# A graph attention layer: the products of V moved to GpSimd, the first body reordered, the last body finished block by block

## The reference

```python
h  = maximum(layernorm(x), 0)
Wh = h @ W
e  = leaky_relu((Wh @ a[:64])[:, None] + (Wh @ a[64:])[None, :], 0.2)
scores    = where(adj > 0, e, -9e15)
attention = softmax(scores, axis=1)
out = x + elu(attention @ Wh)
```

## Time and profile before, and how to read it

| | us |
|---|---|
| median of 3 runs | 683.38 |
| the profiled execution's own time | 682.71 |
| its span, first to last instruction | 680.8 |
| TensorE / VectorE / ScalarE / GpSimd busy | 632.8 / 616.9 / 630.5 / 60.2 |
| DMA | 275.16 MB, mean 404 GB/s |

### The profile page before, as it was taken

How to read it: one execution, slowest core, us unless ns; L and a number is a source line. 1 busy time by engine, 2 the same in 40 slices (tenths; PEclk the granted TensorE clock), 3 DMA queues, 4 the chain that set the end, 5 groups by cost and what they waited for, 6 DMA issues and landing times.

```text
span 680.8 us, 23844 instructions
## 1 busy us (share of the span) xinstructions
PE 632.8 (93%) x10422; PEld 620.1 (91%) x10422; DVE 616.9 (91%) x625; ACT 630.5 (93%) x366; POOL 60.2 (9%) x51
## 2 busy tenths in 40 slices
PE   4769999999998999999999999989898998989895
PEld 4648899999998999999999999989898998989895
DVE  6999899999989899889999999898989989898993
ACT  5998899999999998999999999989898998989981
POOL 5000101011010101011010201010010101001020
PEclk9969999999999999999999999999999999999999
DMA  9997899999999999999999999999999999999970
GB/s 320 426 426 286 328 420 410 422 427 427 428 424 430 428 425 425 429 428 425 427 425 429 428 425 428 426 427 426 427 427 426 427 427 428 425 427 428 424 301 19
DMA packets 24841, 275.16 MB, mean 404 GB/s; under 512 B 3088, under 2 KB 7440, under 8 KB 8432
## 3 DMA queue, kind: packets, MB, share of 16 engines
q1 hardware_dynamic: 22864, 270.67, 94.5%
q0 software_dynamic: 1488, 4.07, 1.6%
q10 hardware_dynamic: 464, 0.07, 0.1%
HBM read 272.70 MB, written 2.10 MB: 404 GB/s over the span
## 4 chain that ended last, share of the span: by engine, by line
DMA 32%; DVE 24%; ACT 20%; PE 14%; issue 10%; DVEq 1%; SPq 0%; ACTq 0%
DMA adj_ring<-in_adj 31%; DVE code L675 15%; ACT work L514 14%; PE psum L916 5%; PE psum L914 5%; ACT work L522 3%; DVE work L688 3%; PE psum L896 3%; DVE code L682 1%; PE psum L954 1%; DMA work<-in_x 1%; ACT trow L497 1%; DVE last_steps L706 1%; DVE last_steps L710 1%; DVE last_steps L699 1%
## 5 line engine op out<-in xcount | busy, mean ns | idle before, releaser
L916 PE MATMUL psum<-V,work 128*128 128x130 f16 x4096 | 492.1, 221 | 0.0
L914 PE MATMUL psum<-V,work 128*128 128x130 f16 x4096 | 491.7, 219 | 0.4 <-DVE work L688 0.4
L514 ACT ACTIVATE work<-trow,Wh 128x4096 int8<-128x4096 f32 x128 | 477.0, 3727 | 1.6 <-DVE code L682 1.6
L914 PEld LDWEIGHTS psum<-V,work 128*128 128x128 fp8e4 x4096 | 400.9, 98 | 0.5 <-issue 0.5
L916 PEld LDWEIGHTS psum<-V,work 128*128 128x128 fp8e4 x4096 | 398.0, 97 | 0.0
L675 DVE TENSOR_SCALAR code<-adj_ring 128x4096 uint8<-128x4096 int32 x128 | 293.0, 2290 | 26.4 <-DMA adj_ring<-in_adj 25.2
L682 DVE SCALAR_TENSOR_TENSOR code<-work,code 128x1024 int32<-128x1024 int32 x128 | 156.5, 1223 | 9.9 <-ACT work L514 7.5
L896 PE MATMUL psum<-identb,code 128*128 128x128 bf16 x2048 | 136.8, 221 | 24.2 <-DVE code L682 20.9
L522 ACT COPY work<-psum 128x1024 int32<-128x1024 int32 x128 | 129.9, 1015 | 26.2 <-PE psum L896 26.2
L896 PEld LDWEIGHTS psum<-identb,code 128*128 128x128 bf16 x2048 | 120.0, 98 | 29.9 <-DVE code L682 21.3
L688 DVE TENSOR_SCALAR work<-work 128x1024 int32<-128x1024 int32 x128 | 88.0, 687 | 3.3 <-ACT work L522 3.2
(11 more groups left out here) (76 smaller groups left out, 150.7 us busy)
## 6 DMA issues: line engine op xcount, KB each, us to landing
adj_ring<-in_adj SPq DMA_DIRECT2D x128, 2048.0 KB, 16.5
work<-in_x SPq DMA_DIRECT2D x4, 512.0 KB, 6.1
last_steps<-in_x POOLq DMA_DIRECT2D x16, 128.0 KB, 6.8
out_y<-last_steps POOLq DMA_DIRECT2D x15, 128.0 KB, 7.8
out_y<-last_steps SPq DMA_DIRECT2D x1, 128.0 KB, 1.9
W<-in_L_gnn_W ACTq DMA_DIRECT2D x2, 16.0 KB, 5.1
Wx<-in_L_gnn_W ACTq DMA_DIRECT2D x2, 16.0 KB, 5.5
a_sb<-in_L_gnn_a ACTq DMA_DIRECT2D x1, 0.5 KB, 4.0
```

The source lines that it names most:

```text
L514: nc.scalar.activation(sign[:, k % 2].bitcast(I8), trow[:, h * UW:(h + 1) * UW], ACT.Sign, bias=(Wh[:, B, 0:1] if isinstance(B, int) else ...
L914: nc.tensor.matmul(sums_of[:, 0:FP], up8[:, j // 2, j % 2], V[:, jb, 0:FP], start=h == 0 and j == 0, stop=False, skip_group_check=True)
L916: last = nc.tensor.matmul(sums_of[:, FP:2 * FP], down8[:, j // 2, j % 2], V[:, jb, FP:2 * FP], start=False, stop=h == 1 and j == HB - 1, s ...
```

## The change

- `products` leaves DVE. POOL, after its minus means, scales `uu` once by `lim` (a new instruction on 128 x 128, semaphore `s_us`) and makes the eight `Y` with `tensor_tensor`, all rounds in a row, with the same wait before round 2.
- PE's sum over the nodes is cut in four steps of 2 matmuls (`total(g)`): one behind the last products of Wh, one behind `t_round(4)`, one behind unit 1's and one behind unit 2's transposes. Unit 3's transposes stand ahead of unit 0's matmuls, unit 5's and unit 6's one unit earlier than before.
- The orders of DVE and ACT in the setup and the first body are redone (below). ACT makes `u` after `step(0, 2)` instead of before.
- In the last body the sums are taken, divided and finished for each block by itself: `finish(b)` on DVE, `copy_lows_of(b)` and `exp_of(b)` on ACT, four stores of 32 KB on SP. `finish(0)` stands between `find_ups` of units 6 and 7; `finish(1)` to `(3)` after the body.

```diff
@@ SP, last body
-                sp.wait_ge(s_res, NI)
-                sp.dma_start(out_i[NI - 1], res[:, :, :].rearrange("p (w b) f -> p w b f", b=2)).then_inc(s_last, 16)
+                for b in range(KE):
+                    sp.wait_ge(z_res, b + 1)
+                    sp.dma_start(out_i[NI - 1, :, b // 2, b % 2], res[:, b]).then_inc(s_last, 16)
@@ POOL
+                pool.wait_ge(s_u, 2)
+                pool.wait_ge(s_lim, 3)
+                nc.gpsimd.tensor_scalar(uu[:, :, :], uu[:, :, :], lim[:, 5:6], None, ALU.mult).then_inc(s_us, 1)
+                pool.wait_ge(s_us, 1)
+                for r in range(NR):
+                    if r == NR - 2:
+                        pool.wait_ge(s_lo, 2 * r)
+                    for h in range(2):
+                        nc.gpsimd.tensor_tensor(Y(r, h), Wh[:, out_of(r), 3:FW],
+                                                uu[:, h, out_of(r)].unsqueeze(2).to_broadcast([P, RR, FE]), ALU.mult)\
+                            .then_inc(s_Y, 1)
@@ ACT, last body
+                def copy_lows_of(b):
+                    act.wait_ge(s_mult, RC + (NI - 1) * BU + KE + b + 1)
+                    nc.scalar.activation(lows[:, b // 2, b % 2],
+                                         acc[b // 2][b % 2].rearrange("p (s l f) -> p s l f", s=2, l=2)[:, :, 1],
+                                         ACT.Copy, scale=1.0 / SPLIT).then_inc(z_low, 1)
+                def exp_of(b):
+                    act.wait_ge(z_neg, b + 1)
+                    nc.scalar.activation(neg[:, b], neg[:, b], ACT.Exp).then_inc(z_exp, 1)
-                copy_lows(NI - 1, 1)
-                negative_part(NI - 1)
+                for b in range(KE):
+                    if b:
+                        copy_lows_of(b)
+                    exp_of(b)
@@ DVE, last body: finish(b), each step waiting for the one before
+   parts = lows + acc (65 x 2);  sums = parts1 * ab + parts0;  fill = (sums_F == 0) * tot;  sums += fill
+   r = 1 / sums_F;  neg = min(sums * r, 0) -> ACT;  hp = max(sums * r, 0);  hp += xg;  res = (neg - 1) + hp -> SP
-                take_sums(NI - 1, 1)
-                divide(NI - 1)
-                result(NI - 1)
+                for b in range(1, KE):
+                    finish(b)
```

More of the change, by code:

```diff
@@ L601, in _ @@
                 step(0, 6)
-                high_parts(3)
+                copy_unit(0, 5)
                 act.wait_ge(s_code, TWO + 6)
                 step(0, 7)
-                copy_unit(0, 5)
+                act.wait_ge(s_code, TWO + 7)
+                step(0, 8)
+                copy_unit(0, 6)
                 act.wait_ge(s_yy, 1)
@@ L626, in body @@
                             copy_lows(i - 1, 1)
-                        if k == 6:
+                        if k == 6 and not last:
                             copy_lows(i, 0)
+                        if k == 5 and last:
+                            copy_lows_of(0)
                         if not (last and k + 3 >= BU):
@@ L777, in _ @@
                 codes(0, 1)
-                dve.wait_ge(s_lim, 3)
-                dve.wait_ge(s_u, 2)
-                products(0)
+                edges(0, 2)
+                edges(0, 3)
                 edges(0, 4)
                 codes(0, 2)
-                products(1)
+                find_ups(0, 0)
                 low_parts(0)
-                find_ups(0, 0)
                 edges(0, 5)
@@ L788, in _ @@
                 codes(0, 3)
+                edges(0, 6)
+                codes(0, 4)
                 find_ups(0, 1)
-                products(2)
+                edges(0, 7)
                 dve.wait_ge(s_total, 1)
@@ L834, in body @@
                             result(i - 1)
-                        if k == 7:
+                        if k == 7 and not last:
                             take_sums(i, 0)
+                        if last and k == BU - 2:
+                            finish(0)
                         if k >= start and not (last and k + lead >= BU):
@@ L888, in t_round, with total @@
                     last.then_inc(s_tp, 1)
+                def total(g):
+                    if g == 0:
+                        pe.wait_ge(s_Whc, 2 * NR)
+                    for g in range(2 * g, 2 * g + 2):
+                        last = nc.tensor.matmul(total_ps.rearrange("p (r f) -> p r f", f=F), ones[:, :],
+                                                Wh[:, g * TR:(g + 1) * TR, 3:FX], start=g == 0, stop=g == JB // TR - 1)
+                    if g == JB // TR - 1:
+                        last.then_inc(s_total, 1)
                 def transpose_unit(i, k):
@@ L935, in _ @@
                 t_round(2)
+                t_round(3)
                 Wh_half_rounds(2)
-                t_round(3)
                 Wh_half_rounds(3)
+                total(0)
                 pe.wait_ge(s_ext, 1)
@@ L945, in _ @@
                 t_round(4)
+                total(1)
+                t_round(5)
                 pe.wait_ge(s_trow, 3)
                 transpose_unit(0, 0)
-                t_round(5)
                 t_round(6)
@@ L952, in _ @@
                 transpose_unit(0, 1)
-                for g in range(JB // TR):
-                    last = nc.tensor.matmul(total_ps.rearrange("p (r f) -> p r f", f=F), ones[:, :],
-                                            Wh[:, g * TR:(g + 1) * TR, 3:FX], start=g == 0, stop=g == JB // TR - 1)
-                last.then_inc(s_total, 1)
+                total(2)
                 transpose_unit(0, 2)
+                total(3)
+                transpose_unit(0, 3)
                 pe.wait_ge(s_trow, JB // TR)
                 multiply_unit(0, 0, first=True)
-                transpose_unit(0, 3)
                 transpose_unit(0, 4)
```

124 lines of the change are left out of this document (72 added, 52 removed).

## The result

The changed kernel takes 687.38 us, the median of 6 runs (686.33 to 689.94), beside 682.49 (681.22 to 683.46) for the kernel before on the same chip: a ratio of 1.0077, 95% interval 1.0065 to 1.0089. It is slower by 4.9 us. The profiled execution takes 687.22 with a span of 685.4 us.

A forecast was written before the change was run, and what follows sets the result against it. The adj stream was taken as the bound, held up in the first body by DVE's edges. +7.0 there and -2.0 in the last body gave +5.0: 688.4 us, forecast's own range 684.8 to 691, 8-in-10 range 676.5 to 691.

The forecast's parts named there:

- Exclusion: First body: POOL products and DVE's SBUF instructions never run together, so the move costs DVE 15.7 us for 10.0.
- rival C: First body: exclusion falls partly in DVE's waits for ACT, or the early part is 2 us better; 683.5, chance 0.12.
- L(8): First body: lateness of the adj stream from the end of unit 8's edges; 9.7 us before, forecast 13.5.
- The scaling: First body: POOL's scaling of uu ahead of the products, forecast 0.3 us, bounds 0.2 and 1.0.
- PE behind it: First body: find_ups(0, 2) due at 76.4, PE ends multiply(0, 7) at 102.3 against 94.0, unit 13 8.3 us later.
- L(13): First body: lateness of the adj stream from the end of unit 13's edges; 10.0 us before, forecast +7.0.
- One for one: Kernel's end: a shift of the stream shifts the end about equally, with 11.9 of the last 12.8 us fixed work.
- The sum in steps at nothing: First body: cutting PE's 8.8 us sum over the nodes gains nothing, since PE waits for codes(0, 3) anyway.
- The last body: Behind the last matmul: only block 3 is left, 2.9 us instead of 4.92; saves 2.0, bounds 1.2 and 2.6.
- POOL's own price: First body: eight POOL products at 1.93 us each, 15.4; by the Trainium skill 18.3, the sum 2.6 worse.
- Rival B: First body: POOL's products run beside DVE, change -3.7 there and -2.0 at the end; 677.7 us, chance 0.32.
- Rival D: First body: POOL gets in only when DVE waits, so DVE waits for Y at low_parts; 692 us, chance 0.06.

The follow-up runs named there:

- the dummy load: Kernel before plus 32 POOL tensor_tensor of 260 elements whose results nobody uses, at the times of the products; 693.6 us, ratio 1.0154.
- the fills: Kernel before plus 96 POOL memsets of 260 elements, results unused, where the 32 unused products stood; 683.63 us, ratio 1.0018.

## Why the prediction was right

**The move is +4.9 against a forecast of +5.0** (687.38 against 688.4: the kernel before measured 682.49 beside it and 683.38 ahead of it, 0.9 of the 1.0 between them).

- *Exclusion.* Shown by the dummy load beside the fills, in the changed kernel by `codes` of 2.3 to 3.0, and the other way round by the scaling of 4.04. That `edges` is stopped too was open in the prediction; it is (4.03 at 59.85). The two overlap pairs of the earlier trace rows had pointed the right way.
- *How much stands.* I put all 15.7 of POOL's time on DVE. Counted from the timeline above (and the `codes` at 41.09, 1.31), DVE stands some 12.6 up to the end of edges(8): two `find_ups` 3.5, three `codes` 2.9, `low_parts` 2.8, two `edges` 3.3. The rest has two sources: a product makes DVE stand 1.75 and not 1.93, 14.0 for the eight (an estimate from the 1.74 of either `find_ups`), and 1.4 of that fell in DVE's waits for ACT (0.61 and 0.80). So edges(8) ended at 78.78 and not at 80.4; edges(3) was nearly as replayed (38.9 for 39.3; the three waits of the setup were 3.2 us together, for about 4.2). A part of rival C was there, 1.6 us of L(8).
- *The scaling.* Forecast 0.3 us, bounds 0.2 and 1.0; it took 4.04, since DVE's three `edges` from 34.48 to 41.1 let it in only behind them. The bound was that of its work, and its wait for the ports was left out, though the same text had exclusion as its case. It cost DVE nothing, but it put the products some 3.5 us later.
- *PE behind it.* find_ups(0, 2) was due by 76.4 and ends at 74.84; multiply(0, 7) ends at 101.11 for 102.3. L(13) 17.2 against 10.0 is +7.2, of which I had taken +7.0. That these meet is in part luck: PE had no gap from 74.94 on, so its path counts in full, 8.3 less the 1.2 that it came sooner. The middle that I took between PE's 8.3 and DVE's 5.6 had no ground in a row, and it made up for the 1.6 of standing too many.
- *One for one.* The start of the last `edges` less L(13) lies between 650.1 and 652.1 in all fourteen kernels, while L(13) goes from 7.7 to 20.6: what the first body loses, the end has, to within some 1 us either way.
- *The sum in steps at nothing.* No run takes it out of the changed kernel, so the nothing is not shown. On the old orders, where POOL is not in the way, the traces show 1.0 to 2.2 us of L(13) for it, the medians 0.5.
- *The last body.* Forecast 2.9 behind the last matmul, 2.0 saved; measured 2.7 and, by the span, 1.9. The 1.9 is low by the 0.8 named above. With an end of 4.50 it saves 2.7: 2.2 up to the last issue, and 0.4 because 32 KB land in 1.45 where the one store of all four blocks took 1.86, a term that the prediction didn't have. So the bound of 2.6 was slightly short.
- *A sign that failed.* A longer empty stretch of the stream from about 58 was to be seen. It is no longer than before, only later (0 GB/s from 62 to 64, 217 and 131 beside it; before 0 from 60 to 62, 123 and 66 beside it). The rest of the loss comes later: 98 GB/s from 70 to 72, 57 from 78 to 80, 127 from 86 to 88.
- *POOL's own price.* With 18.3 in place of 15.4 for the eight the sum would be 2.9 worse, not 2.6 as the prediction has it. A lone product takes 1.95, 15.6 for eight: the price from the trace was right.

**What the parts are worth.** The products on POOL +5.6 alone, the new end -2.5, which leaves about +1.8 for the orders (687.4 - 688.1 + 2.5), if the parts add. They don't quite: with the products on DVE the price of the orders is +5.0. They were made for products that hold DVE up nowhere, and with the real ones on POOL they have nothing to collect. **Rival B**, no exclusion, would have been about right in its price (677.7 for a median of 679.3, within its spread), and its condition is false. **Rival D** is real: the scaling of 4.04 is a small case of it, the kernel with the old setup order a full one. In both, DVE's instructions followed without a gap when POOL was ready; but so they did beside the dummy load, which got its turns.

**What stays open.** What decides whether POOL gets a turn, the price of the setup's order by itself, whether another placement of the products on DVE makes the new order pay, and whether the sum in steps gives the 1 to 2 us of its traces in the time. A chain of `edges` for which POOL's products fit into DVE's real waits wasn't tried.

## What to carry to other kernels

Before moving work from VectorE to GpSimd, look for one pair of rows where the two overlap on SBUF and see whether either is longer than its lone duration; if it is, the move is worth about (time off DVE) minus (GpSimd's time), not (time off DVE). Here that is 10.0 minus 14.0, and GpSimd is the slower of the two (1.95 against 1.25 a product); the kernels lost 5.6 in the old orders and 2.4 in the new. Compare the mean duration of each kind of instruction beside and without the other engine; the busy share can't show it, since an instruction that stands counts as busy. The end of a kernel, where nothing covers a chain of small steps, pays for being cut by blocks so that only the last block's chain is left: 2.7 us here in the traces. And ask which engine is next: with the products short, PE's list let the first body gain 2.3 us of its 10.

## What the runs showed of the hardware that I had not expected

- **Turns.** With short two-input instructions always waiting on POOL, each DVE instruction on SBUF pays one of them: +0.42 us on 2.29 and on 1.24 alike.
- **But not always.** A 128 x 128 scaling that takes 0.62 in the kernel with the old setup order, beside an idle DVE, takes 4.04 in the changed one, and one product 9.01 instead of 1.95, while DVE goes from one instruction on SBUF to the next; it was over 1.8 after the last of them, when DVE had come to a reduction out of PSUM.
- **Fills are half harmless.** Beside 96 fills of 128 x 260 only the one-input kinds were longer (+0.13, +0.11); the kernel's 0.2% more is not seen in the lateness of its first body.
- **The last store.** 32 KB land in 1.5 us in most cases and in 3.7 in one, with 4.5 as the largest of the changed kernel's four. That may be a part of the spread of 2 to 4 us between executions of one kernel; it isn't shown, since one execution of each has a trace.
